# Two-step graph layer on one core: in step two, attended rows are updated between the two tiles' logits, and row units between the row products

## The chip, the cores and the metric

One core of a Trainium2 chip runs the whole kernel. The metric is the time of one execution in device microseconds; a kernel's time is the median of its runs. TensorE (PE in the views) multiplies, VectorE (DVE), ScalarE (ACT) and GpSimd (POOL) do the rest, and SyncE (SP) issues the DMAs.

## The reference

Two graph layers with a layer norm behind each. Only the first matters here. It has N = 3327 nodes with 128 features, and does two steps:

```
R = (S + I) / rowsum                       # S = adj
for n in range(2):
    A  = top_p_attention(Xa, W1, W2, W3)   # softmax(q k^T), smallest set of entries with sum 0.9, renormalised
    Xf = R @ Xf
    Xa = A @ Xa
    Z  = Z + Xf @ U1[n].T + Xa @ U2[n].T
h = X + Z
```

## The kernel before

The rows are padded to 26 tiles of 128, taken in 13 pairs p = 0 to 12; each tile's row of 3327 logits is made in 7 chunks of up to 512. Everything is fp32. `layer0` has one loop over the pairs for each step, written out for every engine; the engines meet by semaphores. The first loop does the attention of step one. The second, which the change touches, does the attention of step two and also both hops of the row path (Xf = R @ Xf), spread over its pairs.

The row path goes by units. A unit u is two row tiles; units 0 to 12 are hop 0, 13 to 25 hop 1. `units_of(p, hop)` gives the one or two units whose update belongs to pair p (pairs 0 to 5: two units of hop 0; pair 6: unit 12; later pairs two units of hop 1). One row product (`rows`, L882 to L895) adds up 27 matmuls for one tile in the single PSUM bank `accR`; ScalarE empties it (`copy_rows`, L1212) into `rawR`, and TensorE may begin the next only then. Its weights are a row block of the adjacency (1.7 MB), which SyncE loads into one of two buffers `adj[k]` when the product before last has given it back (L709).

A pair p of step two (`pair_with_rows`, one for each engine) does this on TensorE, in this order:

- `take_rows` (L932), then `attend` for both tiles: transposes of the kept probabilities (L978), ScalarE's copies to `wT` (L1242), products with the rows (L988), and `rowA` (L1251).
- the logits of pair p+2, tile 0 and then tile 1 (L862, copied by ScalarE at L1164).
- `turn_flags(p+1)` (L914 to L917): VectorE's flags of the next pair turned into one row. It waits for `flags_ready` of pair p+1.
- the updates: for each unit of the pair `turn_rows` (transpose of `rawR`, L901), ScalarE's copy to `xT` (L1230), `update_rows` (product with U1, L907), ScalarE's copy to `zsR` (L1235); and then the same for the attended rows (`turn_attended` L1005, copy L1261, `update` L1011, copy L1265 to `zsA`). All share the bank `xz` and the buffer `xT`.
- the four row products of the units of pair p+1 (L888 and L892).

VectorE, in its pair p: `search(p)` (needs ScalarE's exponentials, `e_ready`), `tops(p+1)` for both tiles (L72: maxima over segments of 64; each needs all seven logit chunks of its tile), `assign_slots(p)` (L1448 to L1468, needs the turned flags), a wait for GpSimd's `marks_ready`, `select` for both tiles (L450, L455 and L461, between branches), whose end (`w_ready`, L1487) lets TensorE attend, and in hop 0 `invert_sums` (L1492), which needs both tiles of each unit of the pair to be read from `accR`. So VectorE searches pair p+1 while TensorE is in pair p.

ScalarE does its copies in TensorE's order. The exponentials of pair p+2 (`exps_of`, L1196 and L1208) stand between the copies of the second and the third row product. GpSimd in pair p: q for pair p+2, in hop 0 the scaling of the pair's units, `find_marks(p+1)` (L784, needs the flags of pair p+1), the addition of the row updates to H (L766), and `give_attended(p)`, which adds `zsA` to H (L745).

The loop is partly rolled: on TensorE, ScalarE and GpSimd pairs 0 to 3 are two passes of a loop of two pairs, 4 to 6 are written out, 7 to 10 are again two passes, and 11 and 12 are written out. The row units 23 to 25 come after pair 12.

Of the kernel before, what the change touches and what calls it, by code (L numbers as in the profile page):

```python
# [9 lines left out]
ACT = mybir.ActivationFunctionType  # L10
# [520 lines left out]
def layer0(nc, d, dims, H, ident):  # L531
# [16 lines left out]
    with ExitStack() as ctx:  # L548
# [141 lines left out]
        with nc.Block() as block:  # L690
# [24 lines left out]
            def _(eng):  # L715
# [8 lines left out]
                for step in range(2):  # L724
# [66 lines left out]
                    def pair_with_rows(p, b, rest, hop, next_hop):  # L791
# [7 lines left out]
                        else:  # L799
                            if hop == 0:  # L800
                                for u, s in units_of(p, hop):
                                    scale_rows(u, s)
                            find_marks(p + 1)
                            for u, s in units_of(p, hop):
                                add_rows(u, hop)
                            give_attended(p)
# [35 lines left out]
            def _(eng):  # L842
# [3 lines left out]
                for step in range(2):  # L846
# [35 lines left out]
                    def rows(u, hop):  # L882

                        xf = XR[0] if hop == 0 else XR[2]
                        for k in range(2):
                            eng.wait_ge(adj_loaded[k], (u + 1) * 16)
                            eng.wait_ge(accR_read, u * 2 + k + 1)
                            eng.matmul(accR[:, :], ident[:, :],  # L888
                                       xf[:, bass.ds((u - hop * PAIRS) * 2 + k, 1), :].rearrange("p a n -> p (a n)"),
                                       start=True, stop=False)  # L890
                            for j in range(T):
                                mm = eng.matmul(accR[:, :], adj[k][:, j * P:(j + 1) * P], xf[:, j, :],  # L892
                                                start=False, stop=(j == T - 1))
                            mm.then_inc(accR_ready, 1)
                            eng.drain()  # L895
                            eng.sem_inc(adj_free, 1)
# [170 lines left out]

                    def pair_with_rows(p, b, rest, hop, next_hop):
# [6 lines left out]
                        if rest >= 2:  # L1075
                            logits(p + 2, 0)
                            logits(p + 2, 1)
                        if rest:
                            turn_flags(p + 1)
                        eng.wait_ge(zsA_ready, turn_of(step, p) + 1)  # L1080
                        if rest:
                            update_all_rows(units_of(p, hop), hop)
                            eng.wait_ge(zsR_ready, units_of(p, hop)[-1][0] + 1)
                        turn_attended(p)
                        update(p)
                        if next_hop == 1:
                            eng.wait_ge(hop_done, PAIRS + 2)
# [1397 lines left out]
```

## Time and profile before

| | |
|---|---|
| median of three runs | 2718.82 us (2716.22 to 2723.67) |
| the profiled execution | 2720.61 us |
| its span, first to last instruction | 2718.8 us |
| TensorE busy, share of the span | 2347.7 us, 86% |
| VectorE busy | 2156.6 us, 79% |
| ScalarE busy | 1070.2 us, 39% |
| GpSimd busy | 138.9 us, 5% |
| granted TensorE clock, mean | 0.945 of 2.4 GHz |

Step two's pairs run from 597 to 1514 us of the span. In a timeline row the columns are start, duration, engine, line, operation, what it writes and reads, how often; the bracket is the time the engine sat idle before it and what released it ("issue": nothing that the profile shows). A group's duration covers all its instructions.

### The profile page before, as it was taken

Reading aid. Unit: us, or ns where it says so; the run is one execution under the profiler, and the core shown is the slowest. Engines: PE = TensorE matmul, PEld = TensorE weight load, DVE = VectorE, ACT = ScalarE, POOL = GpSimd, SP = SyncE. Lnnn points to the kernel's source line nnn. Section 1 sums busy time; section 2 is a strip of 40 time slices with the busy share of each in tenths; the row PEclk is TensorE's granted clock in tenths of the full one; section 3 lists DMA queues with packets and bytes.
Section 4 is the critical chain, followed back from the end, with each engine's and each line's share of the span. In section 5 each row is a group of like instructions: output and inputs, shape, how many; then the busy total and the mean of one; then the engine's idle time right before and its main releaser. Section 6 shows DMA issues by size and latency. Waiting matters only on the chain. (4 is left out here: it accounts for less than half of the span.)

```text
span 2718.8 us, 53799 instructions
## 1 busy us (share of the span) xinstructions
PE 2347.7 (86%) x17795; PEld 1980.7 (73%) x17795; DVE 2156.6 (79%) x6687; ACT 1070.2 (39%) x1803; POOL 138.9 (5%) x342
## 2 busy tenths in 40 slices
PE   7999999878888988888887559987999999999985
PEld 2666666657767777766766459976999999999942
DVE  4777777578876878888889687757999999999836
ACT  5666666433333334433432220004433443344323
POOL 0000000101111111000000000000000000000000
PEclk9999999989989999989988769999999999999987
DMA  3000000022222222212222235542343333334220
GB/s 132 2 1 1 1 1 2 1 102 77 97 76 94 100 103 91 99 64 72 100 99 78 70 136 206 212 175 90 110 147 102 135 120 128 127 108 145 80 90 26
DMA packets 57310, 244.88 MB, mean 90 GB/s; under 512 B 6929, under 2 KB 18576, under 8 KB 43344
## 3 DMA queue, kind: packets, MB, share of 16 engines
q1 hardware_dynamic: 57040, 241.99, 25.4%
q8 instruction: 83, 1.36, 0.2%
q14 instruction: 187, 1.53, 0.2%
HBM read 235.15 MB, written 6.82 MB: 89 GB/s over the span
## 5 line engine op out<-in xcount | busy, mean ns | idle before, releaser
L2075 PE MATMUL a_acc<-H,pT 128*128 128x128 f32 x4056 | 548.0, 277 | 11.5 <-ACT a_rows L2107 3.7
L2075 PEld LDWEIGHTS a_acc<-H,pT 128*128 128x128 f32 x4056 | 495.4, 192 | 28.5 <-DVE pT L2209 19.7
L988 PE MATMUL small<-XR,wT 128*128 128x128 f32 x2756 | 373.7, 281 | 33.7 <-ACT wT L1242 33.1
L988 PEld LDWEIGHTS small<-XR,wT 128*128 128x128 f32 x2756 | 339.7, 195 | 49.6 <-ACT wT L1242 49.6
L862 PE MATMUL lg<-kT,qs 128*128 128x512 f32 (+1 forms) x742 | 340.5, 596 | 31.0 <-ACT e L1164 20.7
L72 DVE MAX8 cand<-e 128x8 f32<-128x64 f32 (+3 forms) x1898 | 302.7, 239 | 61.5 <-issue 38.6
L2209 DVE TENSOR_TENSOR pT<-a_tr,a_adjT 128x512 f32<-128x512 f32 (+1 forms) x546 | 316.7, 645 | 20.6 <-PE a_tr L2034 15.5
L892 PE MATMUL accR<-XR,adj 128*128 128x129 f32 x2704 | 322.8, 281 | 0.0
L2034 PE MATMUL a_tr<-ident,prob 128*128 128x128 f32 x2028 | 311.4, 274 | 10.9 <-ACTq L2101 10.9
L892 PEld LDWEIGHTS accR<-XR,adj 128*128 128x128 f32 x2704 | 319.6, 198 | 0.0
L1242 ACT ACTIVATE wT<-tr 128x512 f32<-128x512 f32 (+1 forms) x371 | 206.0, 566 | 238.0 <-PE tr L978 236.8
L2187 DVE CUSTOM_DVE_ANT_0 prob<-a_adj,EB 128x3328 f32<-128x3328 f32 x78 | 282.6, 3623 | 0.0
L862 PEld LDWEIGHTS lg<-kT,qs 128*128 128x128 f32 x742 | 119.0, 194 | 194.0 <-ACT e L1164 148.2
L1164 ACT ACTIVATE e<-lg 128x512 f32<-128x512 f32 (+1 forms) x371 | 206.5, 566 | 114.1 <-PE lg L862 112.2
L2034 PEld LDWEIGHTS a_tr<-ident,prob 128*128 128x128 f32 x2028 | 241.1, 142 | 11.1 <-issue 11.1
L978 PE MATMUL tr<-ident,e 128*128 128x128 f32 x1378 | 211.7, 281 | 36.4 <-DVE scalars L1487 29.7
L2099 ACT ACTIVATE prob<-prob,a_negmax 128x3328 f32<-128x3328 f32 x78 | 239.0, 3064 | 9.1 <-DVE a_negmax L2196 9.1
L978 PEld LDWEIGHTS tr<-ident,e 128*128 128x128 f32 x1378 | 164.4, 144 | 87.3 <-issue 55.8
L1723 PE MATMUL g_sp<-g_adj,H 128*128 128x128 f32 x1352 | 162.7, 283 | 17.1 <-ACTq L1788 17.1
L1723 PEld LDWEIGHTS g_sp<-g_adj,H 128*128 128x128 f32 x1352 | 158.5, 198 | 18.8 <-issue 18.2
L1196 ACT ACTIVATE e<-e,scalars 128x3327 f32<-128x3327 f32 x53 | 162.1, 3060 | 11.3 <-DVE scalars L1551 10.4
L221 DVE SCALAR_TENSOR_TENSOR work<-cand,mid 128x416 f32<-128x416 f32 (+1 forms) x198 | 143.1, 757 | 10.6 <-issue 3.1
(351 smaller groups left out, 2431.1 us busy)
## 6 DMA issues: line engine op xcount, KB each, us to landing
adj<-in_adjT SPq DMA_DIRECT2D x52, 1664.0 KB, 7.1
g_adj<-in_adjT SPq DMA_DIRECT2D x26, 1664.0 KB, 6.8
a_adj<-in_adj SPq DMA_DIRECT2D x26, 1664.0 KB, 6.9
a_adjT<-in_adjT SPq DMA_DIRECT2D x156, 256.0 KB, 3.9
a_adjT<-in_adjT SPq DMA_DIRECT2D x26, 128.0 KB, 4.2
XT<-in_x_t SPq DMA_DIRECT2D x1, 1664.0 KB, 7.4
hT_scratch<-hT SPq DMA_DIRECT2D x1, 1664.0 KB, 11.7
nsT_scratch<-nsT SPq DMA_DIRECT2D x1, 1664.0 KB, 5.3
```

The costliest lines, as they stand in the source:

```text
L72: eng.max(cand[:, n, :], src[:, n * seg:min((n + 1) * seg, width)])
L862: eng.matmul(lg[bank(st, p, k, c)][:, 0:sl.stop - sl.start], qs[k][:, :], kT[:, sl], start=True, stop=True).then_inc(lg_ready, 1)
L892: mm = eng.matmul(accR[:, :], adj[k][:, j * P:(j + 1) * P], xf[:, j, :], start=False, stop=(j == T - 1))
L978: mm = eng.transpose(tr[(k * NC + c) % 2][:, o:o + P], e[b][k][:, j * P:(j + 1) * P], ident[:, :])
L988: mm = eng.matmul(accA[:, :], wT[(k * NC + c - 1) % 2][:, o:o + P], xa[:, j, 0:P], start=(j == 0), stop=(j == T - 1))
L1164: eng.activation(e[b][k][:, sl], lg[bank(st, p, k, c)][:, 0:sl.stop - sl.start], ACT.Copy).then_inc(lg_free, 1)
L1723: mm = eng.matmul(sp[k][:, :], H[:, j, :], adj[q][:, j * P:(j + 1) * P], start=(j == 0), stop=(j == T - 1))
L2034: mm = eng.transpose(tr[g % BANKS][:, (j % 4) * P:(j % 4 + 1) * P], prob[order[n][1]][:, j * P:(j + 1) * P], ident[:, :])
L2075: mm = eng.matmul(acc[:, :], pT[g % RING][:, (j % 4) * P:(j % 4 + 1) * P], H[:, j, :], start=(j == 0), stop=(j == T - 1))
L2099: eng.activation(prob[h][:, :], prob[h][:, :], ACT.Exp, bias=negmax[h][:, :], accum_out=den[h][:, :])
L2187: eng.tensor_tensor_reduce(prob[h][:, :], adj[k][:, :], EB[:, h, :], 1.0, -3.0e38, ALU.add, ALU.max, mx[h][:, :])
L2209: eng.tensor_tensor(pT[g % RING][:, 0:width(c)], tr[g % BANKS][:, 0:width(c)], adjT[:, c * 512:c * 512 + width(c)], ALU.mult).then_inc(pT_ ...
```

## The change

Nothing is added or taken away in the work; the order changes on three engines, in step two alone. TensorE transposes the attended rows between the two tiles' logits and multiplies them behind the second, ahead of the flags. It transposes the first row unit, does the first row product of the next pair, multiplies the first unit, does the second product, and so on with the second unit and the third and fourth product (`rows_and_updates`). ScalarE follows in the same order, with the exponentials between the copy of the second unit's transpose and the read of the third row product. GpSimd adds the attended rows ahead of `find_marks` and no longer last.

```diff
--- before.py
+++ after.py
@@ -800,10 +800,10 @@
                             if hop == 0:
                                 for u, s in units_of(p, hop):
                                     scale_rows(u, s)
+                            give_attended(p)
                             find_marks(p + 1)
                             for u, s in units_of(p, hop):
                                 add_rows(u, hop)
-                            give_attended(p)
 
                     def make_grid():
...
 
+                    def rows_of(u, hop, k):
+
...
+                        mm.then_inc(accR_ready, 1)
+                        eng.drain()
+                        eng.sem_inc(adj_free, 1)
+
                     def rows(u, hop):
...
+                        rows_of(u, hop, 0)
+                        rows_of(u, hop, 1)
...
+                    def rows_and_updates(units, hop, new_units, next_hop):
+
+                        for i in range(2):
+                            if i < len(units):
+                                u, s = units[i]
+                                eng.wait_ge(zsR_ready, u)
+                                turn_rows(u, s)
+                            if i < len(new_units):
+                                if next_hop == 1 and hop == 0:
+                                    eng.wait_ge(hop_done, PAIRS + 2)
+                                rows_of(new_units[i][0], next_hop, 0)
+                            if i < len(units):
+                                update_rows(units[i][0], hop)
+                            if i < len(new_units):
+                                rows_of(new_units[i][0], next_hop, 1)
+
                     def pair_with_rows(p, b, rest, hop, next_hop):
                         take_rows(p)
                         if at(p, PAIRS - 1):
@@ -1074,20 +1093,16 @@
                         attend(p, b, 1)
                         if rest >= 2:
                             logits(p + 2, 0)
+                        eng.wait_ge(zsR_ready, units_of(p, hop)[0][0])
+                        turn_attended(p)
+                        if rest >= 2:
                             logits(p + 2, 1)
+                        update(p)
                         if rest:
                             turn_flags(p + 1)
-                        eng.wait_ge(zsA_ready, turn_of(step, p) + 1)
-                        if rest:
-                            update_all_rows(units_of(p, hop), hop)
-                            eng.wait_ge(zsR_ready, units_of(p, hop)[-1][0] + 1)
-                        turn_attended(p)
-                        update(p)
-                        if next_hop == 1:
-                            eng.wait_ge(hop_done, PAIRS + 2)
-                        if next_hop is not None:
-                            for u, s in units_of(p + 1, next_hop):
-                                rows(u, next_hop)
+                            eng.wait_ge(zsA_ready, turn_of(step, p) + 2)
+                            rows_and_updates(units_of(p, hop), hop,
+                                             [] if next_hop is None else units_of(p + 1, next_hop), next_hop)
...
+                    def copy_rows_of(u, s, hop, k):
+
+                        if hop == 0 and k == 0:
+                            eng.wait_ge(hop_done, u + 1)
+                        eng.wait_ge(accR_ready, u * 2 + k + 1)
+                        if hop == 0:
+                            eng.activation(rawR[s][k][:, :], accR[:, :], ACT.Copy).then_inc(accR_read, 1)
+                        else:
+                            eng.activation(rawR[s][k][:, 0:P], accR[:, 0:P], ACT.Copy,
+                                           scale=inv_sums[:, bass.ds((u - PAIRS) * 2 + k, 1)])\
+                               .then_inc(accR_read, 1)
+                            if k == 1:
+                                eng.drain()
+                                eng.sem_inc(rowR_ready, 2)
+
...
+                    def copy_rows_and_updates(units, new_units, next_hop, p, b, rest):
+
+                        for i in range(2):
+                            if i < len(units):
+                                copy_turned_rows(units[i][0])
+                            if i == 1 and rest >= 2:
+                                exps_of(p + 2, b)
+                            if i < len(new_units):
+                                copy_rows_of(*new_units[i], next_hop, 0)
+                            if i < len(units):
+                                copy_update_rows(units[i][0])
+                            if i < len(new_units):
+                                copy_rows_of(*new_units[i], next_hop, 1)
+
...
@@ -1331,19 +1364,14 @@
                         copy_row(p, b, 1)
                         if rest >= 2:
                             copy_logits(p + 2, b, 0)
+                        copy_turned_attended(p)
+                        if rest >= 2:
                             copy_logits(p + 2, b, 1)
+                        copy_update(p)
                         if rest:
-                            copy_updated_rows(units_of(p, hop))
-                        copy_turned_attended(p)
-                        copy_update(p)
-                        if next_hop is not None:
-                            units = units_of(p + 1, next_hop)
-                            copy_rows(*units[0], next_hop)
-                        if rest >= 2:
-                            exps_of(p + 2, b)
-                        if next_hop is not None:
-                            for u, s in units[1:]:
-                                copy_rows(u, s, next_hop)
+                            copy_rows_and_updates(units_of(p, hop),
+                                                  [] if next_hop is None else units_of(p + 1, next_hop), next_hop,
+                                                  p, b, rest)
```

`rows_of` is one of the two row products of `rows` before, and `copy_rows_of` one of the two copies of `copy_rows`; their bodies are as before.

## Rows read from the trace of the kernel before

**Rows 1.** Windows view: pair 4 alone, and the sum over the thirteen pairs.
```profile
core 0: us, PE busy (x) PEld busy (x) DVE busy (x) ACT busy (x) POOL busy (x), PEclk, DMA share, GB/s
...
895.20:962.80 67.60, 61.19 (x429) 50.69 (x429) 53.56 (x251) 26.63 (x46) 9.93 (x26) 0.97 0.28 102
...
sum 917.20, PE 776.70 PEld 645.67 DVE 767.38 ACT 333.70 POOL 94.20; mean PE 59.75 PEld 49.67 DVE 59.03 ACT 25.67 POOL 7.25
```

**Rows 2.** Timeline of VectorE, pairs 2 to 10: maxima L72, inverses L1492, slots L1460.
```profile
782.60 0.22 DVE L72 MAX8 cand<-e 128x8 f32<-128x64 f32 x1 [6.93 <-issue]
...
825.74 0.16 DVE L1492 RECIPROCAL inv_sums<-rawR 128x1 f32 x1 [6.61 <-ACT rawR L1219]
...
856.66 0.23 DVE L72 MAX8 cand<-e 128x8 f32<-128x64 f32 x1 [0.27 <-issue]
...
895.32 0.16 DVE L1492 RECIPROCAL inv_sums<-rawR 128x1 f32 x1 [0.35 <-ACT rawR L1219]
...
921.42 0.22 DVE L72 MAX8 cand<-e 128x8 f32<-128x64 f32 x1 [0.77 <-issue]
...
937.94 0.16 DVE L1460 SCALAR_TENSOR_TENSOR scalars<-scalars 128x2 f32<-128x2 f32 x1 [1.09 <-issue]
...
956.92 0.16 DVE L1487 RECIPROCAL scalars<-scalars 128x1 f32<-128x1 f32 x1
...
963.12 0.16 DVE L1492 RECIPROCAL inv_sums<-rawR 128x1 f32 x1 [5.39 <-ACT rawR L1219]
...
1267.40 0.22 DVE L72 MAX8 cand<-e 128x8 f32<-128x64 f32 x1 [2.06 <-issue]
...
1337.75 0.22 DVE L72 MAX8 cand<-e 128x8 f32<-128x64 f32 x1 [2.26 <-issue]
```

**Rows 3.** Timeline of TensorE in pair 4, from its flags to the next pair's start.
```profile
927.62 0.38 PE L914 MATMUL small<-ident,pair_flags 128*1 128x128 f32 x2 [0.29 <-issue]
...
928.20 0.42 PE L901 MATMUL xz<-ident,rawR 128*128 128x128 f32 x2
929.08 0.71 PE L907 MATMUL xz<-UT,xT 128*128 128x128 f32 x4 [0.47 <-ACT xT L1230]
...
934.29 0.64 PE L888 MATMUL accR<-XR,ident 128*128 128x129 f32 x2
...
941.88 0.46 PE L888 MATMUL accR<-XR,ident 128*128 128x129 f32 x2 [0.52 <-ACT rawR L1219]
...
948.61 0.46 PE L888 MATMUL accR<-XR,ident 128*128 128x129 f32 x2 [0.46 <-DMA adj<-in_adjT]
...
956.36 0.49 PE L888 MATMUL accR<-XR,ident 128*128 128x129 f32 x2 [1.49 <-DMA adj<-in_adjT]
...
962.77 0.71 PE L932 MATMUL taken<-XR,XT 128*128 128x129 f32 x4
```

**Rows 4.** Timeline of ScalarE in pair 4: the exponentials, first and last.
```profile
948.36 3.06 ACT L1196 ACTIVATE e<-e,scalars 128x3327 f32<-128x3327 f32 x1
...
954.46 1.16 ACT L1208 ACTIVATE cand<-cand,scalars 128x416 f32<-128x416 f32 x2
```

**Rows 5.** Timeline of GpSimd in pair 4: the marks, first and last instruction.
```profile
920.76 0.19 POOL L784 TENSOR_TENSOR pool_gate<-scalars 128x1 f32<-128x1 f32 x1 [22.37 <-DVEq L335]
...
924.37 0.46 POOL L432 TENSOR_SCALAR hits<-hits,scalars 128x24 f32<-128x24 f32 x1 [0.17 <-issue]
```

**Rows 6.** Timeline of TensorE: the start of pair 2, behind the loop's jump.
```profile
754.63 1.22 PE L932 MATMUL taken<-XR,XT 128*128 x4 [4.97 <-issue]
```

**Rows 7.** Timeline of TensorE in pair 8: late flags, then two row products' starts.
```profile
1195.46 0.57 PE L914 MATMUL small<-ident,pair_flags 128*1 128x128 f32 x2 [4.79 <-DVEq L335]
...
1204.72 0.64 PE L888 MATMUL accR<-XR,ident 128*128 x2
...
1213.73 0.48 PE L888 MATMUL accR<-XR,ident 128*128 x2 [0.67 <-ACT rawR L1221]
```

**Rows 8.** Timeline of VectorE: the same instruction of two selections.
```profile
881.19 3.69 DVE L461 SCALAR_TENSOR_TENSOR e<-work,scalars,e 128x3328 f32<-128x3328 f32 x1 [2.63 <-issue]
...
943.97 3.68 DVE L461 SCALAR_TENSOR_TENSOR e<-work,scalars,e 128x3328 f32<-128x3328 f32 x1 [0.68 <-issue]
```

More of the change, by code:

```diff
@@ L880, in logits @@
                             logit(p, k, c)
-                    def rows(u, hop):
[L884 to L896, printed above, removed]
+                    def rows_of(u, hop, k):
+                        xf = XR[0] if hop == 0 else XR[2]
+                        eng.wait_ge(adj_loaded[k], (u + 1) * 16)
+                        eng.wait_ge(accR_read, u * 2 + k + 1)
+                        eng.matmul(accR[:, :], ident[:, :],
+                                   xf[:, bass.ds((u - hop * PAIRS) * 2 + k, 1), :].rearrange("p a n -> p (a n)"),
+                                   start=True, stop=False)
+                        for j in range(T):
+                            mm = eng.matmul(accR[:, :], adj[k][:, j * P:(j + 1) * P], xf[:, j, :],
+                                            start=False, stop=(j == T - 1))
+                        mm.then_inc(accR_ready, 1)
+                        eng.drain()
+                        eng.sem_inc(adj_free, 1)
+                    def rows(u, hop):
+                        rows_of(u, hop, 0)
+                        rows_of(u, hop, 1)
                     def turn_rows(u, s):
@@ L1210, in exp_tops @@
                         eng.sem_inc(e_ready, 1)
-                    def copy_rows(u, s, hop):
-                        if hop == 0:
-                            eng.wait_ge(hop_done, u + 1)
-                        for k in range(2):
-                            eng.wait_ge(accR_ready, u * 2 + k + 1)
-                            if hop == 0:
-                                eng.activation(rawR[s][k][:, :], accR[:, :], ACT.Copy).then_inc(accR_read, 1)
-                            else:
-                                eng.activation(rawR[s][k][:, 0:P], accR[:, 0:P], ACT.Copy,
-                                               scale=inv_sums[:, bass.ds((u - PAIRS) * 2 + k, 1)])\
-                                   .then_inc(accR_read, 1)
-                        if hop:
-                            eng.drain()
-                            eng.sem_inc(rowR_ready, 2)
+                    def copy_rows_of(u, s, hop, k):
[11 more added lines that the diff above has]
+                                eng.sem_inc(rowR_ready, 2)
+                    def copy_rows(u, s, hop):
+                        copy_rows_of(u, s, hop, 0)
+                        copy_rows_of(u, s, hop, 1)
                     def copy_turned_rows(u):
```

## Prediction

> **What bounds the kernel now.** The change touches step two alone, so I read the views there. The windows view, one stretch for each pair, comes first [rows 1]: over the 917 us of the thirteen pairs TensorE is busy 776.7 us (84.7%) and VectorE 767.4 us (83.7%). Neither is the bound by its share, so the question is who waits for whom. The time line of VectorE answers it [rows 2]. Its work for a pair is a chain: search (25.3 us, from the end of a wait at 895.5 to 920.8), the two tiles' maxima and the slots (921.4 to about 938.4), and the selection (to 957.1), some 62 us. It waits for the other engines at two places only. One is the maxima, which need the first tile's logits: 6.93 us at 782.60, 0.77, 2.06 and 2.26 us later, where 0.27 us stands ahead of this instruction even when nothing is missing (856.66). The other is the inverse of the row sums, which in the first hop needs the last row product of TensorE's pair: 6.61, 0.35 and 5.39 us. Less the 0.27 us that are always there, this is 10.9 us at the maxima; the inverses give 12.4 us, so 23.3 us in all. Everywhere else from pair 0 to the end of the step VectorE works or waits for its own instructions. So VectorE's chain is the step's length, and the most that a faster TensorE can give back is 23.3 us.
>
> TensorE's time line of pair 4 [rows 3] shows where its own 67.5 us go. The first tile's logits have released VectorE by 921.42 [rows 2], the second tile's are done when the flags are turned at 927.62, and then come three updates, 928.20 to 934.29: a transpose, a copy by ScalarE, a product, each waiting for the other (the 0.47 us idle at 929.08 is one of five). Four row products follow, started at 934.29, 941.88, 948.61 and 956.36. They take 7.59, 6.73, 7.75 and 6.41 us.
>
> **The change, part by part.** (1) The attended update moves: its transpose stands between the two tiles' logits and its product behind the second. Both engines have the same matmuls and copies to do as before. A row product of 54 passes takes 6.73 us, 0.125 us a pass, so the transpose (2 passes) costs TensorE 0.25 us and the product (4 passes) 0.5 us: 0.75 us ahead of the flags. Their copies go to ScalarE, which is busy 26.6 of the pair's 67.6 us [rows 1]. The change also adds a wait: the first unit's transpose waits until ScalarE has copied the attended product. Product, copy and their signals take about 1.8 us, of which the flags cover 0.6 and the product itself 0.5, so 0.6 to 0.7 us remain; behind TensorE's wait are queued only its row products. Bounds of the whole: 0 where TensorE waits for the flags anyway, 2.5 us with the clock down; I take 1.4 us.
> (2) Each row unit's transpose now stands ahead of a row product and its product behind it. The round trip to ScalarE is hidden by 6.7 us of row product. The two transposes cost 0.25 us each; the update products (0.5 us) fall into the 0.46 to 0.5 us that TensorE waits for ScalarE to empty the one bank of row sums between products [rows 3]. The second row product of a unit also loads while more work runs ahead of it, so waits for its adjacency can only shrink.
> (3) The exponentials of pair p+2 (ScalarE, two of 3.06 and two of their tops in 1.16 us, 948.36 to 955.6 [rows 4]) stay beside the third row product, but start when the second unit's transpose is copied. They hold up the read of the third product: transpose, copy, 7.3 us and the read make 8.6 us (0.5 + 7.3 + 0.8) in place of 7.75. Bounds of the third product: 6.7 (nothing held up) to 9.5 us.
> (4) The new stretch behind the flags: 0.25 + 6.73 + 6.73 + 0.25 + 8.6 + 6.4 = 29.0 us, against 34.6 us now (928.20 to 962.77). The first product counts 6.73 and not 7.59, since with the idle slots gone the clock should not fall there. Net of (1), a pair saves 34.6 − 29.0 − 1.4 = 4.2 us; behind late flags, which cover (1), 5.6 us.
> (5) On GpSimd, adding the attended rows now stands ahead of finding the marks. Behind that wait are queued the marks, which VectorE needs for its selection. The marks took from 920.76 to 924.8, 4.1 us [rows 5], and are wanted at about 938.4 [rows 2]. In the new order the update's copy ends about 1.5 us behind the second logits, the addition takes 0.9 us, and the marks end some 6.7 us behind the second logits. VectorE can be ready for them at the earliest 17 us after the first logits (921.4 to 938.4), which is 10.7 us after the second. Four microseconds are left, so I cost this at nothing; an update later by more than that would cost VectorE a microsecond a pair for each microsecond.
>
> **The sum on VectorE's chain.** Pair 1: TensorE is held by VectorE's flags there; of the 5.6 us I take 5.0, since the longer wait leaves the clock a little lower. Pair 2 starts that much earlier. The 4.97 us that TensorE idles at the loop's jump ahead of pair 2 [rows 6] stay. The wait of 6.6 us at the maxima becomes 1.6 us: gain 5.0. Pair 2 saves 4.2 more, so the last row product ends 9.2 us earlier, and the wait of 6.6 us at 825.74 shrinks by the 4.2: gain 9.2 by then. From here TensorE saves 4.2 us with each pair while VectorE has only small waits to lose, so TensorE runs ahead: pair 3 ends at 881.8 (895.2 − 13.4), VectorE's selection for pair 4 only at about 886. All remaining waits vanish: 0.35 + 0.5 + 5.4 + 0.2 (one like 921.42) + 1.8 + 2.0 = 10.2 us. Gain 19.4 us.
> The profiled execution took 2720.6 us, which is 1.8 us over the span and 1.8 us over the median of 2718.8. So 2720.6 − 19.4 = 2701.2 for its like, and 2718.8 − 19.4 = 2699.4 for the median. What is late next is VectorE everywhere: from pair 4 on TensorE waits for flags and selections.
>
> **The clock.** Where TensorE waited 4.79 us for the flags of pair 9, its granted clock fell to 1.2 GHz behind it: the first row product took 9.01 us in place of 6.73 [rows 7]. The new kernel has such a wait in nearly every pair from 4 on, 2.3 us each. In the second hop VectorE needs 68.3 us for a pair (1267.40 to 1337.75, less the wait of 2.0 us [rows 2]) and TensorE 67.6 − 4.2 = 63.4, so it is hidden; it is not in pair 1, where it can take up to half of the 5.0 and makes the low end of the gain. The Trainium skill says it as a rule (TensorE: Matmul & The Clock Gate, What's actually happening): the throttled state is the default, and activity releases it; by that rule TensorE could fall behind again, but the sum by rows leaves it hidden.
>
> **Rivals.**
> A, a part of the gain. TensorE saves 2 us a pair and not 4.2, since the third product is held 9.5 us and the clock falls after all. Then the wait of 6.6 falls by 2, the next by 4, and the later ones (7 us in pairs 4 to 10) go: gain 2 + 2 + 7 = 11, 2708 us. For it: the one bank of row sums is emptied by ScalarE in order. Against it: five idle slots of 0.47 us do vanish.
> B, no change: VectorE is the bound and waits elsewhere instead, 2719 us. For it: its waits are only 23 of 917 us. Against it: each of them ends with a TensorE row. A rule of the Trainium skill speaks for B (Perfetto Trace Analysis, Identifying the Most-Contended Engine): judge VectorE by its occupancy and TensorE by its weight loads, and work on the most contended one first. By it VectorE (83.7%) stands before TensorE (645.7 of 917 us, 70%), and shortening TensorE's idle slots would give 0; the waits of VectorE in the rows above give 19.
> C, slower. VectorE's selection branches often, and the idle time ahead of the same instruction is 0.68 us at 943.97 and 2.63 us at 881.19 [rows 8]. VectorE and TensorE now run in another phase, so the jumps fall on other moments of the adjacency loads. If all 24 halves of the selections met the long wait, where about six do now, it would be 18 × 1.95 = 35 us, less the gain of 19: 2735 us. It decides from about 11 more long waits on. The Trainium skill has a rule on this (Runtime: NRT & Kernel Launch, Instruction fetch mechanics): a taken branch to a place that isn't loaded has to be fetched by a DMA first. By it the waits depend on what else the DMA engines do at that moment, which the rows can neither show nor deny.
> D, the change doesn't do what it says: ScalarE's queue holds the row product behind the attended copy. Nothing in the rows supports it, and the price is that of B.
>
> **How the numbers follow.** Forecast (gain 15 to 25): 0.60. A (5 to 15): 0.20. B and D: 0.12. C: 0.05. Better than the bound, by shorter branch waits: 0.03. The predicted time is 2699.4. The range goes from 2691 (the full 23.3 us and 4 us of branch waits) to 2712 (A's lower part, gain 7), which leaves out B, C and little more. A measurement can tell about 0.3%, 8 us, from no change. Faster by more than that: 0.60 + 0.14 of A + 0.03 = 0.77; within: 0.06 of A + 0.11 of B and D + 0.01 of C = 0.18; slower: 0.05.
>
> **What would show it.** Right: no wait of VectorE over 2 us for ScalarE's row copies; 1 to 2 us at the maxima that waited 6.93; TensorE's row products of a pair 28 to 30 us from first start to last end; waits of TensorE for VectorE's flags in most pairs from 4 on; marks never awaited. Wrong in step (3): a third product over 9 us. Wrong in (5): idle time ahead of VectorE's selection beyond 1 us. The forecast as a whole is wrong if VectorE's chain from the maxima of 782.60 to those of 1337.75, 555.2 us now and 541 by the sum (19.4 less the 5.0 that lie ahead), is longer than 548.

## The result, and the profile after

The changed kernel takes 2703.6 us, median of 5 runs (2697.6 to 2706.6), against 2718.8 (2716.2 to 2723.7). The ratio is 0.9932, interval 0.9918 to 0.9945, so 15 to 22 us are gained. The forecast was 2699.4, from a gain of 19.4.

The profiled execution took 2697.6 us, the fastest of the five and 6 us under their median. Its span of 2695.8 us is to be read against the span of 2718.8 before, so the traces show 23.0 us where the medians show 15.2. Its page, then the windows view of pairs 1, 2 and 4 (the columns are those of [rows 1]):

```profile
span 2695.8 us, 53797 instructions
PE 2329.1 (86%) x17795; PEld 1969.8 (73%) x17795; DVE 2159.1 (80%) x6687; ACT 1069.1 (40%) x1803; POOL 152.2 (6%) x342
```

```profile
669.42:746.09 76.67, 61.74 (x429) 51.34 (x429) 61.16 (x258) 26.76 (x47) 10.81 (x22) 0.95 0.31 105
746.09:810.14 64.05, 60.75 (x429) 50.66 (x429) 55.48 (x255) 26.76 (x46) 9.70 (x22) 0.98 0.25 92
...
873.15:935.22 62.07, 58.97 (x429) 49.30 (x429) 53.55 (x252) 26.50 (x46) 12.01 (x22) 1.00 0.31 112
```

Pair 4 took 67.51 us from its own start to the next (895.25 to 962.77; the window of [rows 1] is 0.09 wider) and takes 62.07 now, with as many matmuls (429). Pair 1 took 75.44 us and takes 76.67, for the reason given below.

VectorE's time line, changed kernel, at the places of [rows 2]. In this kernel VectorE's lines from 1420 on have moved by 28 (the inverses L1492 are L1520) and TensorE's by 3 or less; the maxima now come in a record with the line ahead of them, L1448, which has their wait:

```profile
774.51 0.06 DVE L1448 MEMSET gate<- 128x1 f32 x1 [0.26 <-issue]
...
810.11 0.16 DVE L1515 RECIPROCAL scalars<-scalars 128x1 f32<-128x1 f32 x1
810.35 0.80 DVE L1520 RECIPROCAL inv_sums<-rawR 128x1 f32 x4
...
1245.73 0.23 DVE L72 MAX8 cand<-e 128x8 f32<-128x64 f32 x1 [0.27 <-issue]
...
1315.27 0.06 DVE L1448 MEMSET gate<- 128x1 f32 x1 [0.15 <-issue]
```

Every wait of [rows 2] is gone: 6.93 us at the maxima of 782.60 became 0.26 at 774.51, and no wait is left of the 6.61 us at the inverses of 825.74: at 810.35 they follow VectorE's own work. From 774.51 to 1315.27 it is 540.8 us. The prediction said 541, in place of 555.2.

For everything below I use one measure. Step two's stretch runs from VectorE's first selection instruction to its last read of turned flags, 597.39 to 1518.45 before and 596.18 to 1496.31 after, and its time is split. Busy is VectorE's busy time in the windows view. The rest comes from its time line, from idle times over 0.15 us: waits at the maxima and inverses, gaps ahead of the selection's instructions L450, L455 and L461 (the branches), and gaps at the three jumps of its loops. What is left over are short gaps that differ little between kernels. All in us, from one execution each:

| kernel | time | stretch | busy | maxima | inverses | branches | jumps |
|---|---|---|---|---|---|---|---|
| before | 2718.8 | 921.1 | 770.3 | 13.8 | 12.6 | 34.3 | 11.6 |
| after | 2703.6 | 900.1 | 773.3 | 1.1 | 0 | 33.6 | 12.1 |

The stretch is 21.0 us shorter: 25.3 us of waits less and 0.7 of branches, but 3.0 us more busy time, 0.5 at the jumps, and 1.6 in short gaps elsewhere. Of these 1.6 some 1.3 are the 0.26 us that stand ahead of the maxima in any case: the records of the kernel before have more of them ahead of the maxima's own line, where the table's 13.8 counts them, and the changed kernel's more ahead of L1448. So some 24 us of waits have really gone, the 23.3 of the prediction.

TensorE's time line of pair 2, changed kernel (L904 is a unit's transpose, L910 its product, L887 the start of a row product, L1008 and L1014 the attended update):

```profile
773.46 0.43 PE L1008 MATMUL xz<-ident,rowA 128*128 128x128 f32 x2 [0.33 <-issue]
...
779.92 0.71 PE L1014 MATMUL xz<-UT,xT 128*128 128x128 f32 x4
780.46 0.38 PE L917 MATMUL small<-ident,pair_flags 128*1 128x128 f32 x2
...
781.18 0.43 PE L904 MATMUL xz<-ident,rawR 128*128 128x128 f32 x2
781.51 0.48 PE L887 MATMUL accR<-XR,ident 128*128 x2
...
788.46 0.39 PE L887 MATMUL accR<-XR,ident 128*128 x2
...
795.23 0.48 PE L887 MATMUL accR<-XR,ident 128*128 x2
...
801.86 0.71 PE L910 MATMUL xz<-UT,xT 128*128 128x128 f32 x4 [0.34 <-issue]
803.59 0.48 PE L887 MATMUL accR<-XR,ident 128*128 x2 [1.02 <-ACT rawR L1233]
...
810.14 0.71 PE L935 MATMUL taken<-XR,XT 128*128 x4 [0.26 <-issue]
```

The same pair before the change:

```profile
788.86 0.38 PE L914 MATMUL small<-ident,pair_flags 128*1 128x128 f32 x2 [0.25 <-issue]
789.44 0.42 PE L901 MATMUL xz<-ident,rawR 128*128 128x128 f32 x2
790.33 0.71 PE L907 MATMUL xz<-UT,xT 128*128 128x128 f32 x4 [0.47 <-ACT xT L1230]
...
794.19 0.66 PE L1005 MATMUL xz<-ident,rowA 128*128 128x128 f32 x2 [0.66 <-ACT XT L1235]
795.32 1.23 PE L1011 MATMUL xz<-UT,xT 128*128 128x128 f32 x4 [0.47 <-ACT xT L1261]
796.34 0.64 PE L888 MATMUL accR<-XR,ident 128*128 x2
804.55 0.48 PE L888 MATMUL accR<-XR,ident 128*128 x2 [0.46 <-ACT rawR L1219]
```

From the flags to the first row product it was 7.48 us (788.86 to 796.34) and is 1.05. The first product took 8.21 us and takes 6.95, though the unit's update product (4 passes at 787.91) now falls into that time. The windows view of the stretches says why: a granted clock of 0.80 before and of 1.00 after.

```profile
796.30:804.50 8.20, 7.79 (x56) 7.60 (x54) 6.03 (x18) 0.66 (x2) 1.30 (x3) 0.80 0.02 4
```

```profile
781.50:788.40 6.90, 6.79 (x60) 6.60 (x59) 6.82 (x55) 0.66 (x2) 3.66 (x10) 1.00 0.01 2
```

(The second line is of the changed kernel.) The fall is there in the rows before the first product: of the same four passes, 0.71 us at 790.33 and 1.23 at 795.32, behind idle slots of 0.47 to 0.66 us. The kernel with the attended move alone (below) has a first product without the update product in it, and it takes 6.66 us. So the round trips cost the pair their idle slots and some 1.5 us more through the clock (8.21 against 6.66). The pair went from 70.9 to 64.05 us.

### The profile page after: what moved, and what is told of

Read it like the earlier page. It is cut to its first block and busy times, and to the rows that moved or that the text cites. A ratio compares the mean times of both kernels' runs of the same rounds, so it can differ in the third digit from the quotient of the medians.

```text
span 2695.8 us, 53797 instructions
## 1 busy us (share of the span) xinstructions
PE 2329.1 (86%) x17795; PEld 1969.8 (73%) x17795; DVE 2159.1 (80%) x6687; ACT 1069.1 (40%) x1803; POOL 152.2 (6%) x342
## 5 line engine op out<-in xcount | busy, mean ns | idle before, releaser
L2103 PE MATMUL a_acc<-H,pT 128*128 128x128 f32 x4056 | 547.8, 277 | 11.6 <-ACT a_rows L2135 3.8
L2103 PEld LDWEIGHTS a_acc<-H,pT 128*128 128x128 f32 x4056 | 495.3, 192 | 28.6 <-DVE pT L2237 19.9
L72 DVE MAX8 cand<-e 128x8 f32<-128x64 f32 (+3 forms) x1898 | 302.9, 241 | 47.5 <-issue 24.6
L2062 PE MATMUL a_tr<-ident,prob 128*128 128x128 f32 x2028 | 311.3, 274 | 10.9 <-ACTq L2129 10.9
L891 PE MATMUL accR<-XR,adj 128*128 128x129 f32 x2704 | 314.0, 276 | 0.0
L891 PEld LDWEIGHTS accR<-XR,adj 128*128 128x128 f32 x2704 | 309.9, 193 | 0.0
```

Source lines behind the costliest of these rows:

```text
L72: eng.max(cand[:, n, :], src[:, n * seg:min((n + 1) * seg, width)])
L2062: mm = eng.transpose(tr[g % BANKS][:, (j % 4) * P:(j % 4 + 1) * P], prob[order[n][1]][:, j * P:(j + 1) * P], ident[:, :])
L2103: mm = eng.matmul(acc[:, :], pT[g % RING][:, (j % 4) * P:(j % 4 + 1) * P], H[:, j, :], start=(j == 0), stop=(j == T - 1))
```

## Experiments

Times are medians beside the kernel before on the same chip, of which the ratio and its interval tell. Five such comparisons put the kernel before between 2718.8 and 2722.4.

### The changed kernel again

> The changed kernel again, as the measure for the next three on the same chip. Both theories: 15 to 22 us under the kernel before. Step two, from VectorE's first selection to the last turned flags (597.3 to 1518.5 before), about 21 us shorter, with no wait of VectorE over 1 us for logits or row sums.

2701.1 beside 2721.6: ratio 0.9927 (0.9913 to 0.9940). Stretch 903.3, which is 17.8 us under the one before, busy 773.9, branches 35.5. The waits are 1.7, one of them 1.33 us at the maxima, where I had expected none over 1. So two executions of one kernel differ by 3 us in the stretch; smaller differences are not read below.

### One move alone

The attended update alone (the change's order of `turn_attended`, `update`, their copies and `give_attended`, on the kernel before):

```diff
                             logits(p + 2, 0)
+                        eng.wait_ge(zsR_ready, units_of(p, hop)[0][0])
+                        turn_attended(p)
+                        if rest >= 2:
                             logits(p + 2, 1)
+                        update(p)
                         if rest:
                             turn_flags(p + 1)
-                        eng.wait_ge(zsA_ready, turn_of(step, p) + 1)
-                        if rest:
+                            eng.wait_ge(zsA_ready, turn_of(step, p) + 2)
                             update_all_rows(units_of(p, hop), hop)
-                            eng.wait_ge(zsR_ready, units_of(p, hop)[-1][0] + 1)
-                        turn_attended(p)
-                        update(p)
```

> The kernel before with the attended part alone: its transpose between the logits, its product behind them, GpSimd adding it ahead of the marks; the row units stay in one block ahead of the row products. TensorE saves about 1.5 us a pair. Theory (only VectorE's waits count): the wait of 6.6 us at the maxima of 782.6 falls by 1.5, the inverse of 825.7 by 1.5, the inverse of 963.1 by some 4.5 (the savings of pairs 3 to 5 add up there), the small waits of pairs 4, 9 and 10 (about 4 us) go: 12 us under the kernel before. Rival (each part's saving counts in every pair, TensorE being the bound): 11 x 1.5 = 16 us. Rival (the move gives nothing, since the flags hold TensorE anyway): 0 to 2 us.

The row units alone (on the changed kernel, the attended update in one piece behind the flags; GpSimd adds it behind the marks):

```diff
                             logits(p + 2, 0)
+                            logits(p + 2, 1)
+                        if rest:
+                            turn_flags(p + 1)
                         eng.wait_ge(zsR_ready, units_of(p, hop)[0][0])
                         turn_attended(p)
-                        if rest >= 2:
-                            logits(p + 2, 1)
                         update(p)
                         if rest:
-                            turn_flags(p + 1)
                             eng.wait_ge(zsA_ready, turn_of(step, p) + 2)
```

> The changed kernel with the attended update put back into one piece behind the flags, and added behind the marks on GpSimd; the row units stay between the row products. TensorE saves about 3.3 us a pair. Theory: 3.3 + 3.3 at the two long waits, 5.4 at the inverse of pair 5 and 4.5 at the small ones: 16 to 17 us under the kernel before, so the two parts alone (12 and 16.5) come to far more than both together (19 to 21). Rival (TensorE is the bound): 11 x 3.3 = 36 us, and the parts add up.

| kernel | time | ratio | stretch | busy | maxima | inverses | branches | pair 2 on TensorE |
|---|---|---|---|---|---|---|---|---|
| attended alone | 2702.3 | 0.9927 (0.9915 to 0.9940) | 903.1 | 771.5 | 5.3 | 2.1 | 33.6 | 66.6 |
| row units alone | 2708.1 | 0.9940 (0.9928 to 0.9953) | 908.0 | 772.1 | 4.2 | 0.4 | 40.1 | 66.9 |

Beside 2721.6, the medians give the attended move alone 19.3 us, the row units alone 13.5, both together 20.5. By the ratios it is 19.9, 16.3 and 19.9, and all three intervals overlap. So the times can't tell the attended move alone from the whole change, and tell the two halves apart only barely; the stretches (903.1 and 908.0) put them in the same order. I expected 12 and 16 to 17. The 12 was wrong: this half alone is worth as much as both, within the noise. Pair 2 with the attended move alone, TensorE's time line:

```profile
780.61 0.38 PE L914 MATMUL small<-ident,pair_flags 128*1 128x128 f32 x2
...
781.33 0.43 PE L901 MATMUL xz<-ident,rawR 128*128 128x128 f32 x2
782.23 0.71 PE L907 MATMUL xz<-UT,xT 128*128 128x128 f32 x4 [0.47 <-ACT xT L1230]
...
784.95 0.39 PE L888 MATMUL accR<-XR,ident 128*128 x2
791.61 0.48 PE L888 MATMUL accR<-XR,ident 128*128 x2 [0.46 <-ACT rawR L1219]
```

It takes 3.1 us off the way from flags to first product (4.34 us in place of 7.48), and with fewer idle slots in a row the first product takes 6.66 us (8.21 before). That is 4.3 us for the pair, and together with pair 1 enough to take 19.0 of the 26.4 us of waits away. That the halves don't add up (19.3 and 13.5 against 20.5) fits the cap of 23.3 us that the prediction named: once VectorE's waits are gone, more time saved on TensorE is worth next to nothing. The attended move alone still leaves 7.4 us of waits, but has 2.4 us less busy time and 1.9 less in branches than the changed kernel's second execution, and the two stretches come out equal (903.1 and 903.3). The row units alone leave waits of 4.6 us, yet lose 5.8 us on the branches: 9 gaps over 1.2 us (22.3 us together) in place of 6 (13.0).

### GpSimd's order as before

```diff
-                            give_attended(p)
                             find_marks(p + 1)
...
+                            give_attended(p)
```

> The changed kernel with GpSimd's order as before (marks, row units, attended rows last). Theory: equal to the changed kernel within 1 us, since the marks are not awaited in either order and the addition to H is not either. Rival (GpSimd's order was part of the gain, or costs some of it): a difference of 4 us or more either way.

2699.3, ratio 0.9917 (0.9904 to 0.9930), stretch 899.0, busy 771.6. By the times this can't be told from the changed kernel. What the trace does show is below, in the point on step (5).

### Who sets the pace: the same work added to TensorE, and to VectorE

To both kernels, 8 idle matmuls ahead of the first product of each unit, then a second search over 1024 of the columns in each tile of step two:

```diff
+                            for _ in range(8 if k == 0 else 0):
+                                eng.matmul(accR[:, :], adj[k][:, 0:P], xf[:, 0, :], start=True, stop=True)
```

```diff
+                        if step == 1 and begun == 0:
+                            segment_tops(eng, e[b][k][:, 0:1024], 1024, find.cand[k], SEG[step])
+                            eng.drain()
```

> The kernel before with 8 more matmuls of 129 columns on TensorE ahead of the first row product of each unit in step two, about 2 us each, 4 us a pair, 50 us of work in all (the sums are started anew behind them, so the result stays). Theory: TensorE paces VectorE at pairs 1 to 5 and 9 to 10, so the time grows by 24 to 30 us, VectorE's waits growing by as much. Rival (TensorE is the bound throughout): 48 to 52 us. Rival (VectorE is the bound throughout): 0 to 5 us.

> The changed kernel with the same 50 us of TensorE work. Theory: TensorE is ahead by 3 to 12 us there, so only the first hop pays: 12 to 16 us over the changed kernel, at most 2 us of it in the second hop. Rival (TensorE is still the bound): 48 to 52 us.

> The kernel before with the maxima of the first 1024 columns taken twice for every tile of step two on VectorE: 16 more instructions of 0.13 us, 2.2 us a tile, 4.4 us a pair, 12 pairs, 53 us. Theory: the 23 us of waits take up about 20 of it, so 30 to 35 us over the kernel before.

> The changed kernel with the same VectorE work. Theory: VectorE is the bound in every pair, so the whole of it counts: 50 to 54 us over the changed kernel, and the changed kernel's lead over the one before is gone (both some 50 us above 2700). Rival (VectorE still waits for others): under 40 us.

| kernel | time | ratio to before | stretch | its stretch against the kernel without |
|---|---|---|---|---|
| before, TensorE longer | 2743.6 | 1.0072 (1.0050 to 1.0094) | 944.1 | +23.0 |
| after, TensorE longer | 2709.5 | 0.9947 (0.9926 to 0.9968) | 909.6 | +9.5 |
| before, VectorE longer | 2745.5 | 1.0086 (1.0064 to 1.0108) | 942.1 | +21.0 |
| after, VectorE longer | 2738.6 | 1.0055 (1.0034 to 1.0077) | 938.5 | +38.4 |

The padding makes TensorE 46.9 us busier before the change (776.5 to 823.4), and VectorE 46.9 before it and 48.2 after it. So before the change each engine passed on about half of its own 47 us: 23 and 21. The parts are less even. Of TensorE's 23.0, 15.2 are waits of VectorE and 6.2 are two loop jumps that came out longer. VectorE's 46.9 shrank by 21.1 us of waits that it filled, and by 10.1 us of branch gaps, which has nothing to do with who waits for whom. Still, each engine's padding reaches the time in part, and that is what it looks like when two engines pace each other, now one and now the other being late. After the change, TensorE's 36.9 us (759.9 to 796.8) cost 9.5 of the stretch, of which 5.1 are longer branch gaps and 3.2 are waits of VectorE, and VectorE's 48.2 cost 38.4, with branch gaps and jumps 13.2 us shorter. So VectorE paces the changed kernel, with little left for TensorE to hold up.

The medians say the same with other sizes, since the profiled execution of the changed kernel was a fast one: +22 and +24 us before the change; after it +3 to +8 for TensorE and +32 to +37 for VectorE, by which of its two medians one starts from. The expectations for VectorE's padding, 50 to 54 us after the change and 30 to 35 before it, were both too high: they took the branch gaps as fixed, and these moved from 33.6 to 23.7 us and from 34.3 to 24.2 with the code. Those for TensorE's, 24 to 30 before and 12 to 16 after, were a little too high as well.

### The inverses taken off VectorE

GpSimd computes them, as a power of −1, when it needs them:

```diff
-                        if hop == 0:
-                            for u, s in units_of(p, hop):
-                                invert_sums(u, s)
...
-                        eng.wait_ge(inv_ready, u + 1)
                         for k in range(2):
+                            eng.wait_ge(accR_read, u * 2 + k + 2)
+                            eng.tensor_tensor(inv_sums[:, bass.ds(u * 2 + k, 1)], rawR[s][k][:, P:P + 1],
+                                              minus_one[:, :], ALU.pow)
```

> The kernel before with the 26 inverses of the row sums on GpSimd (a power of minus one, ahead of the scaling that needs them) and not on VectorE, so that VectorE's wait at the inverses (12.4 us) cannot arise. Theory: it comes back as a wait at the next maxima, since TensorE's pairs set the pace there; 1 to 3 us under the kernel before (0.8 us of work in the two pairs where VectorE is the bound). Rival (a wait removed is time gained): 12 us plus 5 us of work.

> The changed kernel with the inverses on GpSimd. Theory: VectorE is the bound in each pair, so the work taken from it (0.8 us in each of seven pairs) counts: 3 to 6 us under the changed kernel, a little of it lost where TensorE becomes late in pairs 4 and 5. Rival: nothing, as GpSimd's slower instructions hold the scaled rows up.

On the kernel before it gives nothing: 2724.9, ratio 1.0009 (0.9999 to 1.0020). The 12.6 us of waits at the inverses went, and came back at the maxima, which wait 40.2 us in all in place of 13.8. These 26.4 us more also swallowed the 4.8 us of busy time and the 7.2 us of branch gaps and jumps by which VectorE's own chain got shorter in this kernel; the stretch is 922.4. VectorE's time line of that kernel:

```profile
781.47 0.22 DVE L72 MAX8 cand<-e 128x8 f32<-128x64 f32 x1 [8.93 <-issue]
...
850.88 0.22 DVE L72 MAX8 cand<-e 128x8 f32<-128x64 f32 x1 [6.21 <-issue]
...
920.10 0.22 DVE L72 MAX8 cand<-e 128x8 f32<-128x64 f32 x1 [8.51 <-issue]
...
988.00 0.22 DVE L72 MAX8 cand<-e 128x8 f32<-128x64 f32 x1 [7.68 <-issue]
```

The two kinds of wait of [rows 2] are thus one deficit of TensorE, read at two places; a place taken away shows it at the next. After the change the same edit seems to gain a little: 2696.3, ratio 0.9905 (0.9889 to 0.9920), whose interval only just overlaps those of the changed kernel. Its stretch of 891.6 is 8.5 us shorter: 2.9 us of busy time and 7.2 of branches and jumps (38.5 in place of 45.7), while 2.9 us of waits at the maxima came back, since VectorE now catches up with TensorE.

### The inverses on GpSimd, and its order as before

> The changed kernel with the inverses on GpSimd and GpSimd's order as before (marks, row units, attended rows last). Theory: VectorE is the bound, so the 2.7 us by which its instructions were shorter with GpSimd's old order and the 8.5 us of the inverses add up: step two at about 890 us, 1 to 3 us under the kernel with the inverses alone, near 2695 us. Rival (TensorE has become the bound in pairs 3 to 6): no better than the inverses alone.

2691.6, ratio 0.9888 (0.9872 to 0.9904), stretch 890.9. This is the lowest median of a complete kernel in the study, 28.5 us below the kernel before beside it (2720.1), and 9 to 12 below the two medians of the changed one. From the inverses alone (0.9905, stretch 891.6) it can't be told: the intervals overlap.

### No adjacency loads

The changed kernel with the two big blocks loaded once and 8 columns of each row block after. It leaves out the right row sums, not any instruction of the engines:

```diff
-                            eng.dma_start(adj[k][:, :], d["adjT"][bass.ds((q * 2 + k) * P, P), :]).then_inc(adj_loaded[k], 16)
+                            eng.dma_start(adj[k][:, 0:8], d["adjT"][bass.ds((q * 2 + k) * P, P), 0:8]).then_inc(adj_loaded[k], 16)
```

> The changed kernel with the adjacency of the row products loaded once per buffer and after that only 8 of 3328 columns per load, so that 86 MB less move in step two; it leaves out the right row sums (the row products work on the first two tiles' adjacency), not any instruction of the engines. Theory (VectorE's long waits at branches, over 1.2 us, of which the changed kernel has six with 12 us together, come from instructions that have to be fetched while the loads run): they fall to 0.5 to 1.1 us each, step two shortens by 6 to 9 us. Rival (they come from the branches alone): six of them, step two within 1 us of 900 to 903 us. TensorE's waits for the loads vanish in either case and give nothing, since it is ahead.

2691.7, ratio 0.9894 (0.9878 to 0.9910), stretch 889.2. Two of VectorE's longest branch gaps in the changed kernel, and the jump ahead of pair 4:

```profile
676.89 3.69 DVE L461 SCALAR_TENSOR_TENSOR e<-work,scalars,e 128x3328 f32<-128x3328 f32 x1 [2.57 <-issue]
...
817.24 0.06 DVE L1463 MEMSET gate<- 128x1 f32 x1 [6.09 <-issue]
...
1200.15 0.09 DVE L455 MATCH_VALUE_LOAD work<-drops,work 128x8 f32 x1 [2.47 <-issue]
```

The same without the loads (the longest gap of all 44, and the jump):

```profile
675.36 3.68 DVE L461 SCALAR_TENSOR_TENSOR e<-work,scalars,e 128x3328 f32<-128x3328 f32 x1 [1.08 <-issue]
...
811.65 0.06 DVE L1467 MEMSET gate<- 128x1 f32 x1 [2.88 <-issue]
```

Six gaps over 1.2 us became none, branches 33.6 to 24.8 us, jumps 12.1 to 8.8. The stretch is 10.9 us shorter, where I expected 6 to 9. So the long waits of [rows 8] come from the adjacency loads. The DMA view of the 6.09 us gap, 811 to 817.3 of the changed kernel, shows beside them what VectorE may have waited for:

```profile
q1 hardware_dynamic: 144, 1.70, 76.5%
q8 instruction: 1, 0.02, 1.0%
q14 instruction: 1, 0.01, 0.3%
```

One packet of 8 KB on an instruction queue (q14) starts at 815.28, 4.1 us into the gap, when the 1.70 MB of the row block are nearly through, and one of 16 KB (q8) at 815.98. Without the loads the q14 packet of this jump starts 0.9 us into the gap. Of the changed kernel's six long branch gaps five have an instruction packet starting in them, of the other 38 only four. The Trainium skill (Runtime: NRT & Kernel Launch, Instruction fetch mechanics) says that a taken branch to code that isn't loaded is fetched by a DMA before execution goes on. The trace agrees: the long gaps hold such packets and go with the loads. Which engine a packet belongs to, it doesn't say.

## Why the prediction was right, and where it was wrong

**The bound: right.** VectorE's waits were what TensorE could give back, and all 23.3 us of them went; 21.0 us of the stretch came back. The rule of the Trainium skill that the prediction cites for rival B (Perfetto Trace Analysis, Identifying the Most-Contended Engine) is to optimize the engine with the highest occupancy first, which is VectorE here; the padding shows that before the change TensorE set part of the pace, as VectorE did, at 84.7 and 83.7% busy.

**Step (1): mis-sized.** I took 1.4 us from each pair for the attended parts. In pair 2 the way from the pair's start to its flags went from 34.23 to 34.37 us, in pair 4 from 32.37 to 32.91: 0.1 and 0.5 us (0.6 and 0.8 in pairs 3 and 5). The added wait for ScalarE, priced at 0.6 to 0.7 us, isn't there: the first transpose starts 0.72 us behind the flags (780.46 to 781.18), and its record has no idle time.

**Steps (2) to (4): right.** The stretch behind the flags was put at 29.0 us; it is 28.96 (781.18 to 810.14). The four products take 6.95, 6.77, 8.36 and 6.55 us. Behind the third, TensorE waits 1.02 us for ScalarE, by the mechanism of step (3): the read of the third product's bank comes behind the exponentials. ScalarE's time line of the changed kernel:

```profile
798.71 3.06 ACT L1211 ACTIVATE e<-e,scalars 128x3327 f32<-128x3327 f32 x1
...
801.76 1.16 ACT L1223 ACTIVATE cand<-cand,scalars 128x416 f32<-128x416 f32 x2
803.17 0.28 ACT L1233 ACTIVATE rawR<-accR 128x129 f32<-128x129 f32 x1 [0.25 <-issue]
```

Predicted 8.6, measured 8.36; it was 7.68 before.

**The saving of a pair: too small.** Predicted 4.2, measured 5.4 in pair 4 and 6.9 in pair 2. Of pair 4's surplus of 1.2, 0.9 is step (1). Pair 2 has 1.4 more for another reason: I priced all pairs by [rows 3], but pair 2 had the lower clock, with 7.48 us of updates where pair 4 had 6.67 and a first product of 8.21 where it had 7.59. I had the row for the clock behind late flags [rows 7], and didn't look whether plain pairs showed it as well.

**The sum on VectorE's chain: right by two errors.** Pair 2 starts 8.5 us earlier, 7.3 without the 1.2 by which the whole stretch begins earlier; I had said 5.0. Those 7.3 are made where the prediction put them, behind pair 1's flags: from there to pair 2's start TensorE took 42.47 us and takes 35.57. With 6.9 more in pair 2 the wait of 6.61 us at the inverses went altogether, where 2.4 were to be left, and so did the 1.6 us that I left at the maxima. That makes some 24 us of waits where I counted 19.4. But VectorE's busy time rose by 3.0 us, which I had at nothing. And the 21.0 us belong to the fastest of five executions; the second trace has 17.8. So the 19.4 lies between the two traces, and the medians' gain of 15.2 and 20.5 on either side of it: the mechanism is right, the closeness of the number partly luck.

**Step (5): wrong in its price.** The marks are never awaited, as said. What I left out is that GpSimd and VectorE block each other, and with it the 3.0 us of VectorE's busy time. Two pairs of rows of the changed kernel, from VectorE's and GpSimd's time lines:

```profile
928.52 3.69 DVE L461 SCALAR_TENSOR_TENSOR e<-work,scalars,e 128x3328 f32<-128x3328 f32 x1 [0.77 <-issue]
...
932.28 0.52 DVE L1512 TENSOR_TENSOR scalars<-scalars 128x1 f32<-128x1 f32 x1
...
1173.41 0.76 DVE L310 TENSOR_SCALAR scalars<-scalars 128x2 f32<-128x2 f32 x1
```

```profile
929.05 3.74 POOL L766 TENSOR_TENSOR H<-H,XT 128x256 f32<-128x256 f32 x1 [13.84 <-ACT XT L1254]
...
1173.42 0.72 POOL L745 TENSOR_TENSOR H<-H,zsA 128x256 f32 x1 [46.30 <-ACT zsA L1284]
```

GpSimd's addition takes 0.72 us by itself and 3.74 us here, to 932.79, where VectorE's long instruction ends at 932.21. VectorE's next, 0.16 us elsewhere, then takes 0.52, to 932.80. At 1173.41 an instruction that takes 0.22 us elsewhere takes 0.76, to 1174.17, where GpSimd's ends at 1174.14. Over the stretch, take what each of VectorE's instructions takes above the first quartile of its own kind (same line, operation and shape), where that is over 0.08 us. It sums to 2.4 us in the kernel before (14 instructions), 5.8 after (23), 6.5 in its second execution (25) and 3.9 with GpSimd's old order (19). At every one of them a GpSimd instruction was running, though GpSimd is busy only 12% of the stretch. The rise of 3.4 covers the 3.0 us of busy time. The Trainium skill has the rule (SBUF — State Buffer, Who interferes with whom): the two share a port pair that one of them holds for a whole instruction while the other is blocked. The trace agrees with it in both directions. GpSimd's order is about half of the rise or somewhat more (5.8 to 3.9, one execution of each). The rest would come from the new phase, in which the row units' additions meet VectorE's selection, as at 929.05; no run takes that apart.

**TensorE's waits from pair 4 on: wrong as put.** I expected waits for VectorE's flags in most pairs. They are in three: 6.01 us in pair 1, 3.08 in pair 8, 12.07 in pair 11. From the waits view of step two, 596 to 1497 us, for TensorE's weight loads:

```profile
PEld tr L981 <- DVE scalars L1515: 45.3, 11, 12.3
...
PEld small L917 <- DVEq L335: 22.0, 4, 12.3
```

TensorE waits for VectorE, but twice as long for the end of a selection (L1515), which comes before the flags in its pair: 8.1 us in pair 0, as before the change, and the rest nearly all in pairs 6 to 12. Before, these were 13.5 us in 4 waits, and 12.0 at the flags. TensorE did run ahead; I had the wrong place. Pair 1 is the other case. Pair 0 was 8.6 us shorter, so pair 1 began that much sooner against VectorE, and TensorE then stood still 6.01 us for the flags, which depend on VectorE (0.50 before). Behind the flags the updates fell away (8.09 us from flags to product before, 1.55 now), but the clock fell as in [rows 7]: the first product took 8.24 us, at a granted clock of 0.82.

```profile
710.52 0.58 PE L917 MATMUL small<-ident,pair_flags 128*1 128x128 f32 x2 [6.01 <-DVEq L335]
712.07 0.64 PE L887 MATMUL accR<-XR,ident 128*128 x2
720.31 0.39 PE L887 MATMUL accR<-XR,ident 128*128 x2
```

**The rivals.** A (2 us a pair) falls: 5.4 to 6.9 in pairs 2 to 4. B and D fall: the waits went and nothing took their place. C didn't come: 6 long branch waits before and 6 after, 13.0 and 12.1 us. Its mechanism is real all the same: the row units alone have 9, for 22.3 us, and without the loads there are none. Its size may depend on where the phase falls, which no row of before could tell and no run here varied by itself.

## What to carry to other kernels

Where two engines are equally busy, list the places where each waits for the other: their sum caps what an order change can give, and taking one place away without shortening the late engine's work only moves the wait (12.6 us at the inverses came back at the maxima). Round trips between engines cost their idle slots and what the lower clock does to the work behind them, so price them from each pair's own rows. The first half of a hiding scheme may take nearly the whole cap: here the attended update alone gained 19.3 us, which can't be told from the 20.5 of both. And when two executions of one kernel differ by 3 us, take the gain from the medians and the mechanism from the traces.

## What the hardware showed that I had not expected

- Five idle slots of 0.47 to 0.66 us, from 790.33 to 795.32, stood ahead of a row product whose granted clock was 0.80, so partly at the lower of its two levels (1.2 GHz): 8.21 us, where the same product took 6.66 behind three such slots (782.23 to 784.40, attended update alone).
- GpSimd's additions and VectorE's instructions hold each other up: 0.72 became 3.74 us on GpSimd, 0.22 became 0.76 on VectorE.
- The adjacency loads lengthen VectorE's branch gaps from at most 1.08 us to 2.6, and one loop jump from 2.88 to 6.09. And the gaps depend on the code itself: 33.6 us in the changed kernel, 23.7 with one more search in it and 29.7 with the inverses taken out, loads and all. Why adding code and taking it away both help was not settled.
